# A decoder layer: the last half batch of the shared FFN ahead of the experts, and the experts' rows put in place by indirect transfers

## The reference

```python
probs = softmax(xt @ Wg); eidx = argmax(probs); gate = probs[eidx]      # 2048 tokens, 8 experts
pos = (cumsum(oh, axis=0) * oh).sum(-1) - 1                             # place of a token in its expert
keep = pos < C                                                          # C = 256
flat = where(keep, eidx * C + pos, E * C)
xd = zeros((E * C, d)).at[flat].set(xt, mode='drop').reshape(E, C, d)
h = silu(einsum('ecd,edh->ech', xd, W1)) * einsum('ecd,edh->ech', xd, W3)
oe = einsum('ech,ehd->ecd', h, W2).reshape(E * C, d)
out = take(oe, minimum(flat, E * C - 1)) * (gate * keep)[:, None]
shared = silu(xt @ sw1) * (xt @ sw3) @ sw2
return out + shared                                                     # added to x
```

## Time and profile before

| | us |
|---|---|
| median of 3 runs | 1560.96 |
| lowest, highest | 1559.98, 1564.38 |
| profiled execution | 1559.33 |
| its span, first to last instruction | 1557.5 |
| PE busy | 1445.0 (93%) |
| DVE busy | 1188.3 (76%) |
| POOL busy | 1024.0 (66%) |
| ACT busy | 976.1 (63%) |

### The profile page before, as it was taken

How to read it: one execution, slowest core, us unless ns; L and a number is a source line. 1 busy time by engine, 2 the same in 40 slices (tenths; PEclk the granted TensorE clock), 3 DMA queues, 4 the chain that set the end, 5 groups by cost and what they waited for, 6 DMA issues and landing times.

```text
span 1557.5 us, 27023 instructions
## 1 busy us (share of the span) xinstructions
PE 1445.0 (93%) x8617; PEld 1263.8 (81%) x8617; DVE 1188.3 (76%) x2890; ACT 976.1 (63%) x2478; POOL 1024.0 (66%) x1027
## 2 busy tenths in 40 slices
PE   5899999999999999999999998977989897999997
PEld 4778888888878888778888887757888786999996
DVE  7678888887887887788888888787676755577775
ACT  4687777777677788878878787642121224556562
POOL 3787897887877888878988888434121213345455
PEclk9999999999999999999999999998999998999998
DMA  6435534333322433424434334222000004577777
GB/s 208 140 102 169 156 110 129 120 82 111 107 65 60 121 95 90 128 63 109 114 85 127 84 104 129 78 84 62 28 28 28 8 28 152 167 231 223 229 213 238
DMA packets 107964, 179.17 MB, mean 115 GB/s; under 512 B 17014, under 2 KB 38774, under 8 KB 107824
## 3 DMA queue, kind: packets, MB, share of 16 engines
q1 hardware_dynamic: 105072, 168.94, 37.0%
q0 software_dynamic: 2560, 8.25, 1.6%
q10 hardware_dynamic: 192, 0.26, 0.1%
HBM read 98.36 MB, written 33.03 MB: 84 GB/s over the span
## 4 chain that ended last, share of the span: by engine, by line
PE 62%; DVE 14%; ACT 12%; issue 6%; DMA 3%; POOL 2%; SPq 1%; DVEq 0%; POOLq 0%; ACTq 0%
PE bank L470 14%; PE bank L472 13%; PE bank L471 13%; PE bank L522 5%; ACT P L865 5%; PE bank L537 4%; PE bank L488 3%; PE bank L538 3%; PE bank L489 3%; DVE P L1191 2%; ACT PTh L877 2%; PE bank L462 2%; ACT Otmp L871 2%; DVE PTl L1232 1%; DVE Opair L1226 1%
## 5 line engine op out<-in xcount | busy, mean ns | idle before, releaser
L865 ACT ACTIVATE P<-P,mn 128x512 f32<-128x512 f32 (+3 forms) x512 | 284.5, 557 | 205.6 <-DVE mn L1191 201.8
L1636 POOL TENSOR_TENSOR P<-P,ri 128x128 f32<-128x128 f32 (+3 forms) x512 | 360.4, 735 | 30.8 <-DVE ri L1180 30.7
L1191 DVE CUSTOM_DVE_ANT_0 P<-bank,mask 128x512 f32<-128x512 f32 (+3 forms) x512 | 237.0, 481 | 84.1 <-PE bank L489 82.5
L1232 DVE TENSOR_TENSOR PTl<-bank,PTh 128x512 fp32r<-128x512 f32 (+1 forms) x384 | 229.9, 600 | 34.0 <-ACT PTh L877 31.3
L522 PE MATMUL bank<-ident,P 128*128 128x128 f32 x1280 | 201.4, 272 | 2.5 <-POOL P L1636 2.5
L877 ACT ACTIVATE PTh<-bank 128x512 fp32r<-128x512 f32 (+1 forms) x384 | 197.9, 517 | 3.5 <-PE bank L522 0.5
L488 PE MATMUL bank<-KT,QT 128*128 128x256 f32 (+2 forms) x512 | 187.6, 367 | 7.1 <-DVE mn L1191 7.1
L470 PE MATMUL bank<-XT,Wh 128*128 128x512 f32 x384 | 162.8, 424 | 9.2 <-DVE XT L1162 3.5
L537 PE MATMUL bank<-PTh,VS 128*128 128x256 f32 (+2 forms) x512 | 161.1, 326 | 6.8 <-DVE X L1241 2.4
L489 PE MATMUL bank<-KT,QT 128*128 128x256 f32 (+2 forms) x512 | 165.5, 323 | 0.0
L538 PE MATMUL bank<-PTl,VS 128*128 128x256 f32 (+2 forms) x512 | 154.6, 323 | 0.0
(11 more groups left out here) (224 smaller groups left out, 4160.5 us busy)
## 6 DMA issues: line engine op xcount, KB each, us to landing
RW<-in_wf SPq DMA_DIRECT2D x170, 256.0 KB, 3.0
QT<-qh SPq DMA_DIRECT2D x256, 64.0 KB, 2.0
QT<-ql SPq DMA_DIRECT2D x252, 64.0 KB, 2.0
Oraw<-in_wo SPq DMA_DIRECT2D x16, 512.0 KB, 4.7
KT<-KT SPq DMA_DIRECT2D x32, 256.0 KB, 3.0
Wraw<-in_wqkv SPq DMA_DIRECT2D x9, 768.0 KB, 5.0
xnx<-in_ctx SPq DMA_DIRECT2D x24, 256.0 KB, 3.6
saved<-Wh SPq DMA_DIRECT2D x7, 768.0 KB, 3.5
```

What stands on the lines that cost most here:

```text
L865: e.activation(pq, pq, ACT.Exp, bias=mn[:, z, qb:qb + 1], scale=-1.0, accum_out=rs[:, z, qb:qb + 1]).then_inc(a_exp, 1)
L1191: e.tensor_tensor_reduce(P[:, z, off[qb]:off[qb] + k], bank[n % 2][:, 0:k], mask[:, 512 - k:512], -0.125, BIG, ALU.add, ALU.min, mn[:, z, ...
L1232: e.tensor_tensor(pt_part(PTl, part), bank[2 + part][:, 0:128 * n].rearrange("p (m n) -> p m n", n=128), pt_part(PTh, part).bitcast(F32), ...
L1636: e.tensor_tensor(pq, pq, ri[:, z, qb:qb + 1].to_broadcast([128, n]), ALU.mult).then_inc(g_norm, 1)
```

## The change

Item 15 becomes item 7: all eight half batches of the shared FFN run first, then the eight experts. The first split of an expert's set moves from item 6 to item 7, the last expert splits nothing, and the second load and split of the shared set goes. `load_x` moves to slots 51 and 52, the first turns to 55 and 56 (steps 4 and 5 of item 7).

The tiles of X, with the shared FFN in them, are stored to `out` early, two per item at step 3 of the next. Each row scattered to `xd` has nine more columns: a token number (minus 65536) and the eight logits less their maximum. These columns of `xd` are set to zero first, and are loaded back per slot of the experts' lists. Token numbers and gates are worked out from them. For each expert POOL gathers the tokens' rows out of `out` (step 4), DVE multiplies the expert's banks by the gate and adds the gathered rows (step 7), and POOL puts the rows back into `out` (step 2 of the next expert, or at the end). A slot with no token has a number outside of the bounds and is skipped. `oe`, its stores, `gidx`, the final gathers, combines and stores go.

```diff
     for i in range(2):
-        plan(16 * NB - 16, "load_x", i)
-        plan(16 * NB - 14 + i, "expert_turn", 0, i)
+        plan(16 * NB - 13 + i, "load_x", i)
+        plan(16 * NB - 9 + i, "expert_turn", 0, i)
+    plan(16 * NB - 11, "load_slots", 0)
...
+        slot = LG[:, 0:9 * NT].rearrange("p (t c) -> p t c", c=9)
...
         def set_of(x):
-            return 0 if x < 2 * NB - 1 else x - 6
+            return 0 if x < NX else x - NX + 1
...
-            e.activation(trib[:, :], tri[:, :], ACT.Copy).then_inc(a_const, 1)
+            e.activation(trib[:, :], tri[:, :], ACT.Copy, accum_out=code[:, TB:TB + 1]).then_inc(a_const, 1)
...
+            need.wait_ge(d_slot, 16)
+            e.activation(slot[:, :, 1:9], slot[:, :, 1:9], ACT.Exp).then_inc(a_gate, 1)
...
+                            t = 2 * (x - NX) + i
+                            g = G[t % 8]
+                            need.wait_ge(d_g[t % 8], 32 * (t // 8) + 16)
+                            after()
+                            e.scalar_tensor_tensor(g, bank[2 + i][:, :], gk[:, t:t + 1], g, ALU.mult,
+                                                   ALU.add).then_inc(v_oe, 1)
...
+            def number(b):
+
+                need.wait_ge(v_idx, b + 1)
+                e.tensor_scalar(XN[:, :, D:D + 1], code[:, 0:TB].unsqueeze(2), 1.0, float(b * TB * 128), ALU.mult,
+                                ALU.add).then_inc(g_code, 1)
...
+                e.indirect_dma_start(G[k], None, out, bass.IndirectOffsetOnAxis(ap=tok[:, t:t + 1], axis=0),
+                                     bounds_check=NT * 128 - 1, oob_is_err=False).then_inc(d_g[k], 16)
+
+            def put(t):
+                k = t % 8
+                need.wait_ge(v_oe, t + 1)
+                e.indirect_dma_start(out, bass.IndirectOffsetOnAxis(ap=tok[:, t:t + 1], axis=0), G[k], None,
+                                     bounds_check=NT * 128 - 1, oob_is_err=False).then_inc(d_g[k], 16)
...
-            need.wait_ge(a_const, 1)
+            need.wait_ge(a_const, 2)
+            for i in range(TB):
+                e.tensor_scalar(code[:, i:i + 1], code[:, TB:TB + 1], -1.0, 127.0 + 128 * i - FAR, ALU.mult,
+                                ALU.add).then_inc(g_code, 1)
...
+                    if k == 2 and m:
+                        put(2 * m - 2)
+                        put(2 * m - 1)
+                    if k == 4:
+                        gather(2 * m)
+                        gather(2 * m + 1)
+            put(NT - 2)
+            put(NT - 1)
...
-                e.dma_start(xdz[h - 8], Zb[:, 0, :]).then_inc(d_zero, 16)
+                e.dma_start(xdz[h - 8, :, 0:D], Zb[:, 0, :]).then_inc(d_zero, 16)
+                if h == 24:
+                    e.dma_start(xds, Zb[:, 0, 0:9 * NT].rearrange("p (t c) -> p t c", c=9)).then_inc(d_zero, 16)
...
+                    if k == 3 and x:
+                        store(2 * x - 2)
+                        store(2 * x - 1)
```

More of the change, by code:

```diff
@@ L199, in decoder @@
         peak = nc.dram_tensor("peak", (4 * NCTX,), F32).ap()
-        oe = nc.dram_tensor("oe", (NE * CAP, D), F32).ap()
-        G = [XN[:, k, :] for k in range(TB)] + CW + T1
+        G = [work[:, k, :] for k in range(8)]
         d_x = [sem(f"d_x{i}") for i in range(TB + NB)]
@@ L217, in decoder @@
         d_xe = [sem(f"d_xe{i}") for i in range(2)]
-        d_oe = [sem(f"d_oe{i}") for i in range(2)]
+        d_slot, v_tok, v_oe, g_code = sem("d_slot"), sem("v_tok"), sem("v_oe"), sem("g_code")
         d_g = [sem(f"d_g{i}") for i in range(len(G))]
@@ L671, in ffn @@
                 m = set_of(x)
-                if x < NX - 1 or x == NX + NE - 1:
-                    b, half = divmod(x if x < NX - 1 else NX - 1, 2)
+                if x < NX:
+                    b, half = divmod(x, 2)
                     ready = turn_at["route_turn", b, TB - 1]
@@ L766, in tensor_engine @@
                 side_slot(s)
-            for x in range(NX - 1):
+            for x in range(NX):
                 for k in range(8):
@@ L1590, in vector_engine @@
                 split_piece(0, pieces.pop(0))
-            for x in range(NX - 1):
+            for x in range(NX):
                 for k in range(8):
                     side_slot(8 * x + k - 5)
-                    ffn(x, k, x == NX - 2)
+                    ffn(x, k, x == NX - 1)
                     for _ in range(min(2, len(pieces))):
                         split_piece(0, pieces.pop(0))
-            for s in range(8 * (NX - 1) - 5, max(side) + 1):
-                side_slot(s)
-            gates()
+            token_numbers()
             for m in range(NE):
                 for k in range(8):
-                    ffn(NX - 1 + m, k, True)
+                    ffn(NX + m, k, m < NE - 1)
                     if k in (1, 2) and m + 1 < NE:
                         turn_lo(("expert_turn", m + 1, k - 1))
-            todo = list(range(NT))
-            after()
-            for k in range(8):
-                ffn(NX - 1 + NE, k, False)
-                for _ in range((0, 1, 2, 3, 3, 3, 4, 0)[k]):
-                    combine(todo.pop(0))
+                    if m == 0 and k == 2:
+                        gates()
         def gpsimd_engine(e):
@@ L1821, in gpsimd_engine @@
                         split_piece(0, pieces.pop(0))
-            for s in range(8 * (NX - 1) - 5, max(side) + 1):
-                side_slot(s)
             for m in range(NE):
                 for k in range(8):
-                    ffn(NX - 1 + m, k)
-            for t in range(NT):
-                gather(t)
+                    if m < NE - 1:
+                        ffn(NX + m, k)
+                    if k == 2 and m:
[6 more added lines that the diff above has]
+            put(NT - 1)
+            for k in range(8):
+                need.wait_ge(d_g[k], 64)
         def sync_engine(e):
```

150 lines of the change are left out of this document (60 added, 90 removed).

## The result

| | before | after |
|---|---|---|
| median | 1560.47 (4 runs) | 1547.01 (4 runs) |
| lowest, highest | 1558.22, 1564.38 | 1546.03, 1549.6 |
| profiled execution, its span | 1559.33, 1557.5 | 1547.13, 1545.3 |

The ratio is 0.9914, with a 95% interval of 0.9895 to 0.9933. The change gains about 13.5 us where 20.3 were forecast; the time lies inside the stated range of 1535 to 1552, 6.3 above the predicted 1540.7, but just outside the 1536 to 1546 that the forecast gave as its own.

The account below looks back on a forecast made before the run. The prediction took the experts' stage to be bound by PE, so only its waits or lower clock could change. Terms 11.5 + 1.0 + 9.0 - 1.2 = 20.3 gave span 1537.2, median 1540.7; range 1535 to 1552, the forecast's own 1536 to 1546.

Parts of the forecast that it names:

- Step 1: Change from shared half batches to experts: PE's waits of 3.07 and 5.82 and the half clock go, 11.5 us won.
- Rival D: Expert 0's turns still end late, so PE waits and drops its clock: 8 to 11 back, 1550; chance 0.06.
- Step 2: Half batch 6 splits no weights any more, freeing DVE ahead of placing the last batch: 1.0 us won (0 to 1.4).
- Step 3: Tail after expert 7: 37.8 us becomes a last expert of 23.2 plus 5.6 to the end, 9.0 won.
- Step 4: Row numbers for the scatter: batch 0's logits wait longer for POOL's Gl, 1.2 us lost (0.5 to 2).
- Step 5: Small transfers, the zeros for nine extra columns and their load in half batch 7: 2 to 20 us, taken as 4, no cost.
- Rival B: The small load takes 20 us, pushes weight pieces 8 and 9 by some 10, PE waits: about 1551; chance 0.11.
- Step 6: Gathers, scatters and multiply-adds beside the experts: POOL has room, second gather may land 6.8 us after its start; price zero.
- rival C: DVE becomes the bound of the experts if indirect transfers hold it, some 1 us lost per expert: 1548; chance 0.05.
- Rival A: Gathers beside the weight stream exceed 6.8 us and DVE hands PE the excess per expert; at 10.5, 1567; chance 0.07.

Follow-up runs that it names:

- e0: The changed kernel run once more without an edit: 1545.73, ratio 0.9911.
- e1: The kernel before with the new order only; expert stores, final gathers, combines and final stores stay, after the last expert: 1566.09, ratio 1.0046.
- e3: Changed kernel, with SP instead of POOL waiting for the landing of the last puts: 1546.04, ratio 0.9904.
- e5: Changed kernel without the two puts of expert 7 and their waits, so part of the result is left out: 1536.2 (one run).
- e2: Changed kernel, with Gl on POOL ahead of the four small token-code operations and their wait for the trib copy: 1543.44, ratio 0.9886.
- e4: Changed kernel, with the last expert's down products of tile 0 made wholly ahead of those of tile 1: 1544.6, ratio 0.9904.
- e6: Changed kernel, with each expert's gathers at the end of step 7 instead of step 4: 1594.92, ratio 1.021.
- e7: Changed kernel with e2, e3 and e4 together, no other edit: 1542.28, ratio 0.9882.

## Why the prediction was right, and where its sum was off

Of the forecast 20.3, by stage, by the means of the stages above where the spread from run to run asks for it (five profiles of before; of the others, those that have the stage as the changed kernel has it), and by the first two profiles for the transition and the tail (together 16.6; the means 256.54 and 240.38 give 16.2). Transition and tail are parted at the last product of expert 7 before and of expert 6 after, where both kernels have done the same products and turns:

| step | forecast | measured |
|---|---|---|
| attention (no step) | 0 | -0.9 of means (1048.7 to 1049.6), own spread 6.1 |
| 4, logits | -1.2 | -1.15 (6.40 to 7.55, six profiles) |
| 2, placing and splits of half batch 6 | +1.0 | wait 1.42 gone; stage +0.2 (247.89 to 247.72) |
| 1, transition | +11.5 | +12.6 |
| 6, experts | 0 | -0.3, inside the row above |
| 3, tail | +9.0 | +4.0 |
| sum | 20.3 | 14.8 |

The medians say 13.5 (after) and 15.5 (e0). That the time still fell into the stated range is owed to its width: the tail came out longer, and its gain smaller, than the bounds of 5 to 9.5 that each had, and the range had been widened for rivals that didn't occur. Of the two medians of the changed kernel only e0's, 1545.73, lies within 1536 to 1546.

**Step 1** held. At the placing the same product starts 4.41 later than before (1300.55 and 1304.96), and at the last product of expert 7 or 6 it starts 8.15 earlier (1519.74 and 1511.59): 12.6 against 11.5, over the upper bound of 12. It depends on the profile: the other four of the kernel before give 14.2, 11.0, 11.0 and 11.2 by the same count, with 17.1 and three times 10.2 us of half clock from the first turn's wait on where the first has 13.7. Both waits and the half clock behind them are gone, and the loads came 13.3 us ahead of the first turn. That e1 has this without the rest shows that the order does it. Rival D is not seen.

**Step 2.** The wait of 1.42 is there in all five profiles of before and in none with the new order, and Hl (from 1273 to 1301 before, 1278 to 1305 after) takes 422 ns at the mean in place of 645. In the length of the stage the gain doesn't appear. PE's idle time in it did fall, from 25.9 to 24.3 (means of the same five and six profiles, waits over 0.15 us), but the time at half clock in it was 27.0 in place of 25.8, which is 0.6. The stage itself varies by 5 us in one and the same kernel (244.65, with 20.5 of half clock, to 249.72, with 29.9), so where the rest went stays open.

**Step 3** failed in one term above all: what follows the last landing. The sum had 5.6 from PE's last product to the end. Of it the multiply-add, the two issues (1.03 and 1.00, 0.3 apart) and the landing of 2.8 for 2.7 held; the first put started 0.8 behind its multiply-add for 0.3, at +1.6 for +1.1. For "waits and the last instructions" it had 0.5, and what follows the landing takes 4.5: POOL's closing drain of 4.0 comes after the landing, since POOL waits for the landing itself. Together 10.2 in place of 5.6. The last expert took 23.6 for 23.2 (1511.59 to 1535.16), as expert 7 did before (1496.17 to 1519.74): the sum took 1.1 off for two turns, and an expert with turns (24.2 or 24.4) is only 0.6 to 0.9 longer. The drain was there to be read in the kernel before: it ended at 1554.22, beside DVE's last additions (L1471), and the last store was issued at 1554.99 and set the end, so it cost nothing; and the views of busy time don't list it. The question "which engine ends last, and what does its program still do" wasn't put. e3 moves 2.05 of it off the path, and e5 takes it off wholly.

**Step 4** held: four operations in 1.00 and the accumulator's read of 0.19 (0.2 forecast). e2 takes it back.

**Step 5** held: 3.9 for the load, taken as 4, inside its 2 to 20; the zeros took 6.8 with no one waiting. Rival B is not seen: ACT has no wait for a DMA from 1315 to 1345. The 72 KB of zeros in runs of 36 B came to 11 GB/s, while each of the 256 KB writes out of the same tile took 4.0 us, or 66 GB/s. The Trainium skill (DMA: Bandwidth & Descriptors, Specifications) counts transfers under 512 B as read-modify-writes away from line rate: the low rate agrees, though nobody waits for it; that it comes from a read-modify-write no run shows.

**Step 6** held: the stage from the placing to PE's last product is 230.2 to 230.3 in seven profiles with the gathers in step 4, and 229.9 in e1, which has no indirect transfer beside the experts. Sixteen gathers and fourteen puts there cost PE 0.3 us in all. That rules out rival C. The gathers landed in 4.7 and at most 5.4 (forecast 5.3, 6.5). Rival A's price was too high: 2.9 us from landing to product in place of 5.95, and step 3 reached at 9.6 in place of 8.5, leave about 4 more than the 6.8 of margin that the sum counted (3.5 for the seventh, which has no turns ahead of it). So, as an estimate from these runs, a landing of 10.5 would have cost next to nothing.

The Trainium skill (SBUF — State Buffer, Summary: rules for kernel authors) warns of transfers issued from GpSimd under DVE's work while DVE is in its fast modes. The issues of the gathers, amid DVE's work, took 1.06 at the median and 1.17 at most: no sign of it in this kernel, and no run here shows whether DVE was in such a mode.

## What to carry to other kernels

When a change makes another engine the last one, cost that engine's ending as well: whatever it waits for at its end comes ahead of its closing instructions, which no view of busy time lists. Put the final waits on an engine whose ending is short. And before a drift of a few us in untouched code is explained, profile the unchanged kernel several times: here its own spread (6.1 us in one stage) was twice the drift.

## What the runs showed of the hardware

- POOL's closing drain after indirect transfers: 4.0 us behind its last wait (after, e0, e4, e6), or ended 4.0 behind its last issue (e3, e7); 3.8 where it lay beside PE's work (e5). Behind sixteen gathers in a row, without a wait in between on POOL for the landings, it ended 5.8 (before) and 6.3 (e1) after the last issue. What it does in that time, and why more behind many issues, stays open.
- DVE's splits of 128x512 take 0.63 us each with no operation of POOL beside them (three in 1.88, e6) and 1.6 beside POOL's splits (three in 4.76, before). The 43 in e6's experts with no POOL tensor operation beside them are all under 0.70. That DVE's and POOL's splits hold each other up is the likely reason; no run takes POOL's away alone.
- An indirect put of 128 rows starts 0.8 us after the DVE operation that it waits for has ended (e4).
- In the kernel before, the same program had PE at half clock for 10.2 to 26.6 us ahead of the first shared product. Of five profiles the one with 26.6 was the latest (1052.90), but three with 10.2 differ by up to 1.0, and e1 and e5, with 12.8 and 13.0, by 3.3: the clock is a large part of the spread, not all of it.
